# Tile 1's first transposes moved ahead of layer 2 in an fp32 ranking kernel, with GpSimd unpaced in tile 1 and the first ids loaded alone

## The reference

```python
x0 = emb[ids].reshape(ids.shape[0], -1)
x = x0
for i in range(cross_w.shape[0]):
    s = x @ cross_w[i]
    x = x0 * s[:, None] + cross_b[i] + x
h = jax.nn.relu(x0 @ w1 + b1)      # 1664 -> 1024
h = jax.nn.relu(h @ w2 + b2)       # 1024 -> 512
h = jax.nn.relu(h @ w3 + b3)       # 512 -> 256
logit = jnp.concatenate([x, h], axis=1) @ out_w + out_b
return jax.nn.sigmoid(logit)
```

## Time and profile before

| what | value |
| --- | --- |
| median of 3 runs | 537.11 us (536.67 to 539.26) |
| the profiled execution | 536.77 us, of which its span is 535.0 us |
| PE busy | 469.5 us, 88% of the span |
| PEld busy | 435.6 us, 81% |
| POOL busy | 379.1 us, 71% |
| DVE busy | 184.6 us, 35% |
| ACT busy (its DMA issues not counted) | 104.9 us, 20% |
| PE idle, 59.6 to 64.2 us | 4.62 us |

### The profile page before, as it was taken

The page is one execution under the profiler, slowest core; times in us unless marked ns, Lnnn a source line. Parts: engine busy times, 40 slices in busy tenths (PEclk is TensorE's granted clock), DMA queues, the critical chain, the costliest instruction groups (busy, mean ns, idle before and its releaser), DMA issues.

```text
span 535.0 us, 11277 instructions
## 1 busy us (share of the span) xinstructions
PE 469.5 (88%) x2876; PEld 435.6 (81%) x2876; DVE 184.6 (35%) x383; ACT 104.9 (20%) x194; POOL 379.1 (71%) x407
## 2 busy tenths in 40 slices
PE   0088599999898999899898999989899898999997
PEld 0088389898888989798897989889798887989996
DVE  5464523314142322424232241423233142323325
ACT  6495501101011110111111020111011011101111
POOL 5777667577777777777777777777777777777720
PEclk9999999999999999999999999999999999999999
DMA  7992111011111111111111111111111111111100
GB/s 230 229 365 80 25 23 29 23 30 26 30 30 27 30 30 28 28 30 31 26 31 28 29 29 29 29 28 29 30 28 28 31 26 31 28 28 29 28 10 2
DMA packets 21730, 25.17 MB, mean 47 GB/s; under 512 B 11335, under 2 KB 12322, under 8 KB 21666
## 3 DMA queue, kind: packets, MB, share of 16 engines
q0 software_dynamic: 12800, 13.13, 11.9%
q1 hardware_dynamic: 6800, 11.01, 6.0%
q10 hardware_dynamic: 2066, 0.31, 0.3%
HBM read 24.41 MB, written 0.01 MB: 46 GB/s over the span
## 4 chain that ended last, share of the span: by engine, by line
PE 51%; ACTq 12%; POOL 10%; issue 9%; ACT 6%; DMA 6%; DVE 5%; POOLq 0%; DVEq 0%
PE l_bank L714 39%; ACTq L389 11%; POOL x_raw L341 10%; DMA x_raw<-in_L_rec_emb,idx 5%; PE x_bank L714 4%; PE x_bank L730 3%; PE h_bank L758 3%; ACT xT_hi L402 2%; ACT w_hi L359 2%; DVE x_raw L520 2%; ACTq L386 1%; DVE xT_lo L527 1%; PE l_bank L789 1%; ACT h_bank L369 1%; DVE h2T_lo L532 1%
## 5 line engine op out<-in xcount | busy, mean ns | idle before, releaser
L341 POOL DMA_INDIRECT x_raw<-in_L_rec_emb,idx x400 | 378.3, 946 | 132.1 <-issue 104.4
L714 PE MATMUL l_bank<-w_hi,xT_hi 128*128 128x342 f32 (+1 forms) x624 | 145.2, 333 | 8.0 <-DVE xT_lo L527 7.9
L714 PE MATMUL l_bank<-w_lo,xT_hi 128*128 128x342 f32 (+1 forms) x624 | 137.9, 321 | 0.0
L714 PE MATMUL l_bank<-w_hi,xT_lo 128*128 128x342 f32 (+1 forms) x624 | 137.9, 321 | 0.0
L714 PEld LDWEIGHTS l_bank<-w_hi,xT_hi 128*128 128x128 f32 x624 | 103.4, 190 | 12.8 <-DVE xT_lo L527 11.4
L714 PEld LDWEIGHTS l_bank<-w_lo,xT_hi 128*128 128x128 f32 x624 | 106.8, 190 | 0.0
L714 PEld LDWEIGHTS l_bank<-w_hi,xT_lo 128*128 128x128 f32 x624 | 106.5, 190 | 0.0
L527 DVE TENSOR_TENSOR xT_lo<-x_bank,xT_hi 128x512 fp32r<-128x512 f32 (+1 forms) x66 | 38.2, 578 | 164.5 <-ACT xT_hi L402 164.5
L402 ACT ACTIVATE xT_hi<-x_bank 128x512 fp32r<-128x512 f32 (+1 forms) x66 | 33.5, 507 | 262.7 <-PE x_bank L730 199.7
L730 PE MATMUL x_bank<-identity,x_raw 128*128 128x128 f32 x208 | 34.9, 280 | 44.1 <-DVE x_raw L520 27.1
L730 PEld LDWEIGHTS x_bank<-identity,x_raw 128*128 128x128 f32 x208 | 25.2, 142 | 53.1 <-issue 50.5
(11 more groups left out here) (90 smaller groups left out, 289.4 us busy)
## 6 DMA issues: line engine op xcount, KB each, us to landing
ids<-in_L_rec_emb SPq DMA_DIRECT2D x1152, 0.2 KB
ids<-in_L_rec_emb ACTq DMA_DIRECT2D x896, 0.2 KB
w_raw<-in_L_rec_w SPq DMA_DIRECT2D x18, 512.0 KB, 21.3
x_raw<-in_L_rec_emb,idx POOLq DMA_INDIRECT x400, 2.8
b_rows<-in_L_rec_b SPq DMA_DIRECT2D x1, 512.0 KB, 9.4
b_rows<-in_L_rec_b SPq DMA_DIRECT2D x1, 256.0 KB, 7.5
ids<-in_r_ids SPq DMA_DIRECT2D x1, 208.0 KB, 2.7
b_rows<-in_L_rec_b SPq DMA_DIRECT2D x1, 128.0 KB, 8.0
```

The costliest lines, as they stand in the source:

```text
L341: pool.indirect_dma_start(out=dst, out_offset=None, in_=emb, in_offset=rows).then_inc(landed, 16)
L714: done = pe.matmul(bank[:, 0:b - a], x[:, k, :], w[:, k, a:b], start=(k == 0 and n == 0), stop=(k == last_k and n == 2))
```

## The change

Four things are changed.

- On TensorE, x(1,0) is transposed right after layer 1's output of tile 0, ahead of layer 2 of tile 0. Between layer 2's halves now stand all of tile 1's first group (two chunks, the transpose of x(1,1), two chunks). Behind the second half follow one chunk of group 1, the transposes of `h2(0)` and of x(1,2), and the other two chunks of group 1. From group 2 on tile 1 is as before.
- ScalarE and VectorE follow: `x_hi(1,0)` goes ahead of the last three weight splits, `x_hi(1,1)` ahead of the last one, and likewise `make_whole` and `x_lo`. ScalarE's fetches of 8, 12, 4 and 16 rows, which were spread between `x_hi(1,0)`, `h2_hi(0)`, `x_hi(1,1)` and `x_hi(1,2)`, now all stand behind the last split and ahead of `x_hi(1,2)`.
- GpSimd waits for `chunk_done` from tile 2 on only (SLACK goes), and the wait at field 2 holds at tile 2 as well.
- The ids of the first 8 fields of tile 0 come in a DMA of their own (4 KB) ahead of the DMA of the others, with their own semaphore.

```diff
-    SLACK = {1: 2}
+    FIRST_PACED = 2
...
-            sync.dma_start(ids[:, :], r_ids.rearrange("(p t) f -> p (t f)", p=P)).then_inc(ids_loaded, 16)
+            by_row = r_ids.rearrange("(p t) f -> p (t f)", p=P)
+            sync.dma_start(ids[:, 0:FIRST], by_row[:, 0:FIRST]).then_inc(first_ids_loaded, 16)
+            sync.dma_start(ids[:, FIRST:TILES * F], by_row[:, FIRST:TILES * F]).then_inc(ids_loaded, 16)
...
-                if f == 2 and t > 2:
+                if f == 2:
                     pool.wait_ge(h2_transposed, t - 1)
...
-                        if t > 0 and f % FPK == 0 and f // FPK not in NOT_PACED:
-                            pool.wait_ge(chunk_done, max(1, PACED * t - BEHIND[f // FPK] - SLACK.get(t, 0)))
-                        if t > 1:
+                        if t >= FIRST_PACED and f % FPK == 0 and f // FPK not in NOT_PACED:
+                            pool.wait_ge(chunk_done, PACED * t - BEHIND[f // FPK])
+                        if t >= FIRST_PACED:
                             other_engines_turn(t, f)
...
                 h1_hi(0)
-                for n in LATE:
+                x_hi(1, 0)
+                for n in LATE[:-1]:
                     split_hi(n)
+                x_hi(1, 1)
+                split_hi(LATE[-1])
...
             first_step()
             act.wait_ge(sp_idx_ready, 1)
-            for t in range(1, TILES - 1):
+            fetch(ACT_SHARES[0])
+            fetch(ACT_SHARES[1])
+            h2_hi(0)
+            fetch(ACT_SHARES[2])
+            rest_of_step(1)
+            for t in range(2, TILES - 1):
                 step(t)
...
+                make_whole(1, 0)
                 dve.wait_ge(consts_summed, 1)
...
                 h1_lo(0)
-                for n in LATE:
+                x_lo(1, 0)
+                make_whole(1, 1)
+                for n in LATE[:-1]:
                     split_lo(n)
+                x_lo(1, 1)
+                split_lo(LATE[-1])
...
+                    l2_out(0)
+                    make_whole(1, 2)
+                    h2_lo(0)
...
+            dve.wait_ge(first_ids_loaded, 16)
+            to_indices(0, FIRST)
             dve.wait_ge(ids_loaded, 16)
-            to_indices(0, FIRST)
             to_indices(FIRST, TILES * F)
...
                 transpose_h1(0)
+                transpose_x(1, 0)
+                l2(0, range(0, HB))
+
+            def begin_second():
+
+                l1(1, 0, slice(0, 2))
+                transpose_x(1, 1)
+                l1(1, 0, slice(2, None))
+                l2(0, range(HB, K2))
+                l1(1, 1, slice(0, 1))
+                transpose_h2(0)
+                transpose_x(1, 2)
+                l1(1, 1, slice(1, None))
+                rest_of_step(1, 2)
```

More of the change, by code:

```diff
@@ L217, in splits_done @@
             return 2 * (n + 1)
+        first_ids_loaded = sem("first_ids_loaded")
         ids_loaded = sem("ids_loaded")
@@ L445, in step @@
                 x_hi(t, 1)
[L446 to L455, removed]
+                rest_of_step(t)
             def last_step(t):
@@ L476, in cross_hi, with rest_of_step @@
                                ACT.Copy).then_inc(cross_hi_ready, 1)
+            def rest_of_step(t):
+                fetch(ACT_SHARES[3])
+                x_hi(t, 2)
+                if t in SP_TILES:
+                    sp_place(t)
+                if t in ACT_TILES:
+                    act_place(t)
+                fetch(ACT_SHARES[4])
+                x_hi(t, 3)
+                fetch(ACT_SHARES[5])
+                h1_hi(t)
             first_step()
             act.wait_ge(sp_idx_ready, 1)
-            for t in range(1, TILES - 1):
+            fetch(ACT_SHARES[0])
[4 more added lines that the diff above has]
+            for t in range(2, TILES - 1):
                 step(t)
@@ L645, in step @@
             def step(t):
[L646 to L649, removed]
+                if t > 1:
+                    begin(t)
+                    make_whole(t, 2)
+                else:
+                    l2_out(0)
+                    make_whole(1, 2)
+                    h2_lo(0)
+                x_lo(t, 2)
+                make_whole(t, 3)
+                x_lo(t, 3)
                 l1_out(t)
@@ L849, in begin, with rest_of_step @@
                 l1(t, 0, slice(-ahead(t), None))
-            def step(t):
-                begin(t)
-                for g in range(1, NG):
+            def rest_of_step(t, first_g):
+                for g in range(first_g, NG):
                     l1(t, g, slice(0, -ahead(t)))
@@ L859, in step @@
                 l3(t - 1)
+            def step(t):
+                begin(t)
+                rest_of_step(t, 1)
             def last_step(t):
@@ L897, in _ @@
             first_step()
-            for t in range(1, TILES - 1):
+            begin_second()
+            for t in range(2, TILES - 1):
                 step(t)
```

## The result

The changed kernel takes 540.75 us (median of 6 runs, 540.2 to 542.26) against 538.36 us for the kernel before (6 runs, 536.67 to 539.26): a ratio of 1.0055 with a 95% interval of 1.0033 to 1.0077. A second comparison, with other runs, gave 1.0058 (1.0031 to 1.0085). So it is slower, by about 3 us. The number forecast, 539.5 us, lies 1.25 us under the median, and "no change on the slow side" was the wrong side of the line: the interval lies above 1, and its middle above 0.5%. The 1.25 us are the difference between the two medians of the kernel before, 537.11 of the three runs that the forecast was built on and 538.36 of all six.

The account below looks back on a forecast made before the run. The prediction took the start of x(2,0), set in tile 1 by ScalarE's fetches, to bound the kernel. Its terms, 1.6 + 1.7 - 0.9 = +2.4 us, gave 539.5 us on the median, range 537.4 to 541.2.

Parts of the forecast that it names:

- What decides: Time follows the start of x(2,0) one for one; ScalarE's fetches, not TensorE's 4.62 us hole, set tile 1's group 2.
- TensorE's reorder: Tile 1 on TensorE: x(1,1) transposed at 62.3, then TensorE needs x(1,2) at 73.3 and waits.
- ScalarE's reorder: Tile 1: fetches start at 65.15 behind the last split, `x_hi(1,2)` comes at 81.9 against 80.28: +1.6 us.
- The clock: TensorE idles from 73.3 to 83.3, falls to 1.2 GHz at the head of tile 1's group 2: +1.7 us.
- The first ids: Tile 0's first ids in their own DMA bring the first gathers earlier: -0.9 us, bounded by 0 and 1.3.
- Rival (b): Early ids don't reach TensorE, the eighth gather lands at 25.9 as before: +3.3, 540.4 us; chance 0.2.
- GpSimd: Unpaced in tile 1, its lead is waited away at field 16 of tile 2, for x(2,0): 0.
- The sum: Whole kernel: 1.6 + 1.7 - 0.9 = +2.4 us, giving 539.5 us on the median, +0.45%.
- Which side of the line: Whole kernel: "no change" within 0.5% (2.7 us), chance 0.47; slower 0.46; faster 0.07.
- (c): No loss: ScalarE's loads short (0.6 a gap), early ids pass in full: +0.8, 537.9 us; chance 0.17.
- (d): Faster: TensorE's hole counted; with `x_hi(1,2)` by 73, 4.62 and 1.7 us come back: 530.8 us; chance 0.07.
- (e): Longer low clock, or `h1_hi(1)` held behind ScalarE's last fetch of the step: 541.3 us and above; chance 0.06.

Follow-up runs that it names:

- the faster kernel of the experiments: The changed kernel without ScalarE's fetches in tiles 1 and 2 (GpSimd gathers tile 3's last field instead): 532.08 us, ratio 0.9862 to the kernel before.

## Why the prediction was right, and where it was not

- **What decides.** Right: the time follows x(2,0), and tile 1's x(2,0) is set by ScalarE's issues, not by TensorE's hole. Over all eleven profiles x(2,0) goes from 88.73 to 103.45, and from there to the end it is 438.8 to 441.8 us in each. The two kernels without the fetches show the rest from both sides: with the fetches the reorder loses 0.55%, without them it gains 1.2%.
- **TensorE's reorder.** Right to 0.2 us, once the 0.56 us by which everything came earlier are taken off: x(1,1) transposed at 61.69 (62.3 - 0.56 = 61.7), the hole from 72.9 on (73.3 - 0.56 = 72.7).
- **ScalarE's reorder.** The start of the train was right (64.52; 65.15 - 0.56 = 64.6). Its length was mis-sized: 17.24 us to `x_hi(1,2)` instead of 16.7. This is the step that failed: "I take 1.0 for each of the three gaps", 3.0 us together. They took 1.20, 0.72 and 1.63 us, 3.55 together; the issues took what they had before, 13.64 for 13.72. The load of 16 rows in the changed kernel (least, median and longest duration in ns, the same for one load, then its start) and in the kernel before:

```profile
L390 ACTq TENSOR_LOAD <-at_bytes x1: 1511/1511/1511, 74.8 to 74.8; - x1
...
L386 ACTq TENSOR_LOAD <-at_bytes x1: 1194/1194/1194, 73.6 to 73.6; - x1
```

A load's time goes with its rows, and I had taken the median of all loads for every one. In the kernel before 4 rows take 0.49 to 0.64 us, 8 rows 0.72 to 0.74, 12 rows 0.96 to 1.17, 16 rows 1.19 to 1.24. But the rows alone would not have mended the sum: the gaps of the same three loads in the kernel before were 1.12, 0.58 and 1.28 us, 3.0 together. What I missed is that they take longer in the new train, the load of 16 rows above all, which now stands straight behind issues: 1.51 us here, 1.30 to 1.33 in the four other profiles with this train, where the three gaps sum to 3.3 to 3.5 us. Why they do, no run shows. The term was +2.0 (1.48 at `x_hi(1,2)` and the 0.56 that came earlier), not +1.6.

- **The clock.** Right in kind, a little small: 1.88 us for 1.7. That this loss was hidden before and is on the path now is what the trace with the busy TensorE shows.
- **The first ids.** -0.9 was taken, -0.56 is in this pair of profiles, and about -0.9 at x(0,0) across all eleven profiled kernels. The 4 KB landed in 1.9 us, not near the 1.4 that I leaned on. The Trainium skill ("DMA: Bandwidth & Descriptors", section "Anatomy of one DMA") gives its fixed 2.0 us for DMAs issued from GpSimd; taken over to SyncE's as an estimate, it is nearer to the 1.9 measured for 4 KB than my bound was. The 0.5 us estimated from it between 4 and 208 KB is less than the 0.8 by which the ids' landing moved (2.7 to 1.9). Rival (b), that the early ids don't reach TensorE, is out.
- **GpSimd.** Right: 0. All its lead was waited away in tile 2.
- **The sum.** With the terms as the profile pair has them, -0.56 + 2.04 + 1.88 = +3.36 at x(2,0), for +2.4 forecast: the train is 0.4 of the difference, the first ids 0.3, the clock 0.2. A further 0.5 us came behind x(2,0), where I expected nothing; it is spread over tiles 2 to 15 (from x(2,0) to x(15,0) 402.09 us instead of 401.59) and I have no cause for it. The medians moved by 2.4 us, the ratio says 0.55%, about 3 us.
- **Which side of the line.** The prediction drew the line between "no change" and "slower" at 0.5% (2.7 us), and its sum was 0.3 us short of it. The train's gaps alone were 0.5 us too small, and so the likelier side, 0.47 to 0.46, was the wrong one, by a hair. The line was too wide as well: the measured interval reaches 0.22% to either side, so the +0.45% forecast would have been told from none. Rivals (c) and (d) did not come about, (e) in part: the low clock was longer, 4.2 us of work for 3.4. (d)'s mechanism, with the train cut, is the faster kernel of the experiments.

## What to carry to other kernels

When an engine's idle hole is to be filled, look one step further down for the wait that the hole has been hiding behind: here TensorE reached it 0.56 us early in spite of a hole of 4.62 us, so that filling the hole could give nothing as long as ScalarE's issues set that point. DMA issues are work of the engine that issues them and show in no busy time; count them per tile (here 64 and their loads, some 28 us of a 31 us tile) and ask where they can start. Here a reorder began them 2.2 us later (64.52 for 62.34), which brought the end of tile 1's train 1.5 us later, and the same reorder pays once the fetches are left out of tiles 1 and 2.

## What the runs showed of the hardware that I had not expected

- The clock of TensorE fell after short waits too, in some executions and not in others: after 1.93 us in tile 0 in one profile of the changed kernel and not after 1.91 in the other, with x(0,3) 1.49 us later for it. Runs of the kernel before range from 536.67 to 541.9 us, and the low clock goes with the long ones: in the second comparison the five with a mean granted clock of 0.997 took 536.88 to 537.05 us, the seven at 0.990 and less 538.1 to 540.28. That such falls make up all of the spread isn't shown.
- How long the low clock lasts behind a wait does not follow the wait: behind 10.22 us it was low for 4.2 us of work, behind 8.88 us for 6.2.
- The time of a TENSOR_LOAD on ScalarE's queue goes with the registers that it fills, from 0.49 us for 4 to 1.71 for 20, but not with them alone: 16 took 1.19 to 1.51.
